# Four graph layers: edge attributes turned in the GCN stages, reciprocals turned instead of sums, query scores as rows, another order of steps

## The chip, the cores and the metric

The kernel runs on one core of a Trainium2 chip. The metric is device time in microseconds, lower is better. The kernel before takes 4228.95 us (median of 3 runs, 4228.57 to 4229.52). A profiled execution has every instruction of the five engines: PE (TensorE), DVE (VectorE), ACT (ScalarE), POOL (GpSimd) and SP (SyncE, which here only issues DMAs).

## The reference

50,000 nodes of 128 features and 25,000 edges, sorted by destination, pass through four layers, each followed by a residual and a layer norm. Only the last two are touched in their arithmetic:

```
# layer 2 (8 heads)
q, k, v = x @ Wq + bq, x @ Wk + bk, x @ Wv + bv
score = einsum('ehd,ehd->eh', q[dst], k[src]) / sqrt(HD) + edge_attr_32 @ We + be
exp_s = exp(score - segment_max(score)[dst])
out = segment_sum(exp_s / (segment_sum(exp_s)[dst] + 1e-8) * v[src]) @ Wo + bo
x = layernorm(x + layernorm(out + x) * gamma + beta)
# layer 3 (4 heads)
alpha = (q_s[dst] + k_s[src] + edge_attr_64 @ We3) / sqrt(C) + gate * edge_weight
ex = exp(leaky_relu(alpha) - segment_max)
x = layernorm(x + segment_sum(ex / (denom[dst] + 1e-16) * v[src]) + bias)
```

Layer 1 is a graph convolution of three rounds (gather, sum by destination, matrix product, relu).

## The kernel before

The program is a row of stages with a barrier of all engines between them. The first two (to about 1800 us) treat all nodes and layer 0. Then come three **graph stages** (`for layer in range(3)`, L1488) and two **attention stages** (`for kind in (2, 3)`, L1713). All five walk over the same 49 chunks of 512 edges (`G_CH`), the tile being 128 partitions x 512 columns of float32.

In a graph stage POOL gathers the source rows of a chunk by four indirect DMAs (L1563), PE turns them (L368, four 128x128 transposes against the identity), DVE runs the segmented scan (L1655) and adds the node's own row, ACT applies the relu, PE multiplies by the next weight. The order there is written out by hand: one iteration `t` issues the work of several chunks, each at its own distance behind `t`.

An attention stage is a software pipeline. `Line` holds five sets of buffers (`RING = 5`). A step such as `maximum` is a function of the chunk L with a **place**, a number in the table `plan`. Every engine sorts its own steps by place + lag x L and issues them in that order, whatever their cost (`Line.run`):

```
order = [(place + self.lag * L, k, L, step) for k, (place, step) in enumerate(self.queue) for L in range(G_CH)]
for when, k, L, step in sorted(order, key=lambda o: o[:3]):
    step(L)
```

So the table alone decides what stands before what on an engine, and it says nothing of when it runs: that is decided by semaphore waits at the head of the instructions. With a lag of 138 (kind 2) or 137 (kind 3), places that differ by one lag are one chunk apart.

The steps of kind 2, in the order of one chunk: `load` (SP), `gather` of source and own rows (POOL, eight indirect DMAs, L886), `residual` (POOL, two additions, L1812 and L1813), `turn_x` (PE: turns source rows, own rows and the edge attributes `ea`), `copy_xT` (ACT, three copies PSUM to SBUF), `products` (PE: keys and queries), `copy_z` (ACT), `qk` (DVE), `scores` (PE: edge term L1895, then sum over heads L1897), `maximum` (DVE: running maximum L919 and what the exponentials need), `exps` (ACT, L929 and L931), `values` (PE, L1887), `sums` (DVE: message, running sum `den` L943, running sum `num` L946), `turn_sums` (PE: turns `num`; four small products with the turned query `xdT` for the scores of the next layer, L1922; four for the rows of `den`, L951), `divide` (DVE), `turn_o` (PE: the quotient turned back), `copy_oT` (ACT), `rows_o` (PE, times Wo, L374), two layer norms on DVE and ACT (`d`, `e`), `store` (SP), `turn_q` and `copy_q` (the result turned for the next chunk's query scores).

Kind 3 has one gather a chunk (four DMAs), no second norm, and at its end `scatter` (POOL, four indirect DMAs to `out`, L1828). Its ACT switches its function table twice a chunk: square root for the norm, exponential for the weights.

PSUM has eight banks of 2 KB a partition, `K[0]` to `K[7]`; a step that writes a bank waits for the reader of its last use.

## Time and profile before

| | us |
|---|---|
| median of 3 runs | 4228.95 |
| profiled execution | 4232.34 |
| its span in the trace | 4230.3 |
| graph stages, from first memset to the start of kind 2 | 1809.7 to 2687.4 |
| kind 2, from its first DMA to the first DMA of kind 3 | 2687.4 to 3578.6 |
| kind 3 | 3578.6 to 4230.3 |
| granted TensorE clock, mean over the span | 0.738 |

A timeline row gives start, duration, engine, line, operation, and in brackets how long the engine sat idle before it and who ended that. Distances from one start to the next are shorter than the durations, since neighbours overlap at their ends.
### The profile page before, as it was taken

How to read it: one execution, taken by the hardware profiler on the slowest of the kernel's cores; microseconds unless marked ns; L12 is line 12 of the kernel's file. 1: busy time of each engine (PE TensorE's matmuls, PEld its weight loads, DVE VectorE, ACT ScalarE, POOL GpSimd, SP SyncE). 2: the span in 40 equal slices, each digit the busy share in tenths (PEclk: the TensorE clock that was granted, in tenths of full speed). 3: DMA queues.
4: the chain of work that ended last, by engine and by line, in shares of the span. 5: the costliest groups of instructions: out<-in, count | busy, mean ns of one | idle time of the engine just before them, and what ended most of it. 6: DMA issues, size and time to landing. Idle time of an engine off the chain costs nothing. (4 is left out here: it accounts for less than half of the span.)

```text
span 4230.3 us, 49000 instructions
## 1 busy us (share of the span) xinstructions
PE 2899.9 (69%) x12128; PEld 1933.6 (46%) x12128; DVE 3478.3 (82%) x8156; ACT 2509.0 (59%) x5535; POOL 2568.4 (61%) x2300
## 2 busy tenths in 40 slices
PE   5877777777742788745465455478888885777775
PEld 3555455554530344444455344345555554444443
DVE  4999999999986888668788699677777785788886
ACT  3777777777751666635545444356666564565555
POOL 6666666666501666167577577587666651666664
PEclk9899999999975777667657655677777785655655
DMA  4887766665534888457667566322222221333331
GB/s 117 182 184 192 188 180 193 183 192 188 174 138 122 253 249 254 150 176 245 220 199 242 196 184 198 94 73 69 64 66 66 69 55 38 102 87 91 91 94 49
DMA packets 390823, 624.83 MB, mean 148 GB/s; under 512 B 125015, under 2 KB 206080, under 8 KB 390542
## 3 DMA queue, kind: packets, MB, share of 16 engines
q1 hardware_dynamic: 320782, 508.68, 40.0%
q0 software_dynamic: 69760, 113.02, 11.4%
q8 instruction: 101, 1.65, 0.2%
q14 instruction: 180, 1.47, 0.1%
HBM read 338.14 MB, written 287.17 MB: 148 GB/s over the span
## 5 line engine op out<-in xcount | busy, mean ns | idle before, releaser
L1563 POOL DMA_INDIRECT gs_g<-table_xw,slot_idx x588 | 616.8, 1049 | 319.5 <-issue 261.9
L886 POOL DMA_INDIRECT gs_t<-table_x,slot_idx x392 | 418.4, 1067 | 302.3 <-issue 198.9
L493 POOL DMA_INDIRECT gs<-x,src_idx x200 | 223.9, 1119 | 292.2 <-DMA xd_rows<-gd 211.0
L368 PE MATMUL ps<-ident,gs_g 128*128 128x128 f32 x588 | 143.4, 391 | 369.1 <-DMA gs_g<-table_xw,slot_idx 369.0
L1258 POOL DMA_INDIRECT slot_idx<-node_map,src_idx x200 | 242.1, 1211 | 196.9 <-DMA slot_idx<-node_map,src_idx 103.6
L481 POOL DMA_INDIRECT node_map<-slot_no,end_idx x200 | 302.6, 1513 | 60.9 <-issue 60.0
L1601 ACT ACTIVATE hT_g<-u_g 128x512 f32<-128x512 f32 x147 | 92.4, 629 | 391.5 <-DVE u_g L1662 391.1
L1828 POOL DMA_INDIRECT out<-x_t,end_idx x196 | 205.5, 1049 | 169.4 <-ACT x_t L339 116.7
L368 PEld LDWEIGHTS ps<-ident,gs_g 128*128 128x128 f32 x588 | 95.9, 200 | 408.0 <-issue 344.6
L1655 DVE TENSOR_TENSOR_SCAN agg_g<-same_seg,agg_g,ps 128x512 f32<-128x512 uint8 x147 | 187.8, 1278 | 93.1 <-PE ps L368 92.5
L493 POOL DMA_INDIRECT gd<-x,dst_idx x200 | 218.7, 1093 | 60.9 <-issue 59.7
L1887 PE MATMUL ps<-xsT_t,Wv 128*128 128x512 f32 x196 | 156.1, 890 | 132.3 <-DVE msg_t L939 132.1
L886 POOL DMA_INDIRECT own_t<-table_x,own_idx x196 | 200.9, 1025 | 59.7 <-issue 59.7
L1650 DVE SCALAR_TENSOR_TENSOR own_g<-bs_row,root,own_g 128x128 f32<-128x128 f32 x588 | 166.7, 345 | 27.6 <-DMA own_g<-table_xw 26.7
L1979 ACT COPY xsT_t<-ps 128x512 f32<-128x512 f32 x49 | 28.7, 585 | 249.3 <-PE ps L368 249.3
L374 PE MATMUL ps<-WS,hT_g 128*128 128x128 f32 x784 | 163.1, 378 | 9.6 <-ACT xw_g L1609 9.3
L594 ACT ACTIVATE x_b<-v_b,nm,rs 128x128 f32<-128x128 f32 x392 | 156.6, 495 | 17.1 <-DVE nm L769 17.1
L368 PE MATMUL ps<-ident,own_g 128*128 128x128 f32 x588 | 146.5, 398 | 29.0 <-DVE own_g L1650 28.0
L594 ACT ACTIVATE x_b<-s_b,nm,rs 128x128 f32<-128x128 f32 x392 | 156.7, 496 | 14.1 <-DVE nm L769 14.1
L374 PEld LDWEIGHTS ps<-WS,hT_g 128*128 128x128 f32 x784 | 154.9, 293 | 11.8 <-issue 11.2
L1952 ACT COPY xsT_t<-ps 128x512 f32<-128x512 f32 x98 | 56.4, 576 | 172.8 <-PE ps L368 172.8
L594 ACT ACTIVATE x_b<-t_b,nm,rs 128x128 f32<-128x128 f32 x392 | 157.4, 510 | 0.0
(365 smaller groups left out, 9936.3 us busy)
## 6 DMA issues: line engine op xcount, KB each, us to landing
table_xw<-xw_b SPq DMA_DIRECT2D x147, 512.0 KB, 4.6
table_x<-x_b SPq DMA_DIRECT2D x98, 512.0 KB, 2.8
own_g<-table_xw SPq DMA_DIRECT2D x147, 256.0 KB, 4.2
x_in<-x SPq DMA_DIRECT2D x49, 512.0 KB
y_g<-table_x SPq DMA_DIRECT2D x49, 512.0 KB, 4.8
table_xw<-xw_g SPq DMA_DIRECT2D x98, 256.0 KB, 2.8
out<-y_g SPq DMA_DIRECT2D x49, 512.0 KB, 4.2
pen_t<-pen_row SPq DMA_DIRECT2D x98, 256.0 KB, 4.1
```

The lines of the kernel that those rows point to most:

```text
L368: last = nc.tensor.transpose(to[0:width, j * P:(j + 1) * P], t[:, j * width:(j + 1) * width], ident[:])
L374: last = nc.tensor.matmul(to[:, j * D:(j + 1) * D], tT[:, j * P:(j + 1) * P], W[:], start=True, stop=bias_row is None)
L481: pool.indirect_dma_start(out=node_map, out_offset=bass.IndirectOffsetOnAxis(ap=end_idx[:, t:t + 1], axis=0), in_=slot_no[:, t:t + 1], in_ ...
L493: pool.indirect_dma_start(out=to[k % 3][:, j * D:(j + 1) * D], out_offset=None, in_=x, in_offset=bass.IndirectOffsetOnAxis(ap=of[:, n:n + ...
L594: last = nc.scalar.activation(to[:, k * D:(k + 1) * D], of(k), ACT.Identity, scale=r[:, n, k:k + 1], bias=b[:, n, k:k + 1])
L886: pool.indirect_dma_start(out=self.B[L % RING][g][:, t * D:(t + 1) * D], out_offset=None, in_=table, in_offset=bass.IndirectOffsetOnAxis(a ...
L1258: pool.indirect_dma_start(out=slot_idx[:, t:t + 1], out_offset=None, in_=node_map, in_offset=bass.IndirectOffsetOnAxis(ap=src_idx[:, t:t + ...
L1563: pool.indirect_dma_start(out=gs[c % 6][:, j * D:(j + 1) * D], out_offset=None, in_=tables[layer], in_offset=bass.IndirectOffsetOnAxis(ap= ...
L1650: V.scalar_tensor_tensor(out=blk, in0=bs_row[layer][:], scalar=root4[:, k:k + 1], in1=blk, op0=ALU.mult, op1=ALU.add).then_inc(S("own_bias ...
L1655: V.tensor_tensor_scan(agg[t % 3][:], same_seg[:, t * CH:(t + 1) * CH], T_X[t % 2], agg[(t - 1) % 3][:, CH - 1:CH], ALU.mult, ALU.add).the ...
L1828: pool.indirect_dma_start(out=out, out_offset=bass.IndirectOffsetOnAxis(ap=end_idx[:, k:k + 1], axis=0), in_=B[L % RING]["x4"][:, t * D:(t ...
L1887: nc.tensor.matmul(K[3], (Wv if kind == 2 else Wv3)[:], B[L % RING]["xsT"][:], start=True, stop=True).then_inc(S("v_ps"), 1)
```

## The change

1. **Edge attributes.** In the three graph stages every third iteration also takes one chunk of the edge attributes: SP loads both kinds (32 and 64 wide) side by side, PE turns them in four transposes (banks 6 and 7, unused there), ACT copies them out with a stride, SP stores the turned chunk to `eaT_d`. The attention stages load `eaT` straight from it; their turn on PE, copy on ACT and the buffers `ea` are gone.
2. **Reciprocals turned (kind 2).** `turn_sums` makes only the rows of `den`. DVE forms the reciprocal (`divisor`), ACT widens it from 32 to 512 columns (`widen_rd`), PE turns it (`turn_rd`), and DVE multiplies it with `num` where that lies, straight into `xsT` (`divide`). The turn of `num`, `turn_o` and `copy_oT` are gone.
3. **Query scores as rows.** Eight instructions (L1922) in `turn_sums` and a copy on DVE (L2062) become `query` (one product of 4x512), `keep_q` (ACT) and `store_q` (SP). The turning of all scores at the start of kind 3 is gone.
4. **Residual.** In kind 2 the two additions go from POOL to DVE.
5. **Banks.** In kind 3 the edge scores and the values have two banks each.
6. **Both plans** get other places; the lags stay.

```diff
+            ea_in = [... f"ea_in_g{layer}_{k}", [P, SUB, 96] ... for k in range(3)]
+            ea_t = [... f"ea_t_g{layer}_{k}", [96, CH] ... for k in range(2)]
+            def ea_chunk(t):
+                return t // 3 if t % 3 == 1 and 0 <= t // 3 < N_E else None
...
+                        k = ea_chunk(t)                      # SP
+                            if k >= 3:
+                                sp.wait_ge(S("ea_ps"), k - 2)
+                            sp.dma_start(ea_in[k % 3][:, :, 0:32], ea_rows(ea32, k))...
+                            sp.dma_start(ea_in[k % 3][:, :, 32:96], ea_rows(ea64, k))...
...
+                        k = ea_chunk(t - 2)                  # PE, ahead of the layer's product
+                            pe.wait_ge(S(f"ea_in{k % 3}"), 32 * (k // 3 + 1))
+                            for j in range(SUB):
+                                last = nc.tensor.transpose(T_E[k % 2][0:96, j * P:(j + 1) * P], ea_in[k % 3][:, j, :], ident[:])
...
+                            nc.scalar.copy(ea_t[k % 2].rearrange("f (p j) -> f j p", j=SUB), ...)
...
-                "turn_x": (38, "xsT_ps xdT_ps eaT_ps"), "copy_xT": (66, "xsT xdT eaT"), "products": (84, "k_ps q_ps"),
+                "turn_x": (-37, "xsT_ps xdT_ps"), "copy_xT": (62, "xsT xdT"), "products": (78, "k_ps q_ps"),
...
-                **ln_plan("f", 474, 490, 516, 522), "scatter": (540, "")}
+                **ln_plan("f", 429, 473, 479, 602), "scatter": (612, "")}
...
-                        sp.dma_start(b["ea"].rearrange("p (j f) -> p j f", j=SUB), hop.rows(ea, L, 0))...
+                        sp.dma_start(b["eaT"][0:width, :], turned[:, L * CH:(L + 1) * CH])...
...
-                        turn(pe, K[2], b["ea"], width).then_inc(S("eaT_ps"), 1)
...
+                        @step("scores_e")
+                            step.due_dma(pe, "ea_in", L)
+                            step.due(pe, "M", L, 1)
+                            step.due(pe, "dz", L, 1)
+                            nc.tensor.matmul(K[2], we2_rep[:], b["eaT"][:], start=True, stop=False)
...
+                        @step("turn_rd")
+                            step.due(pe, "rd_wide", L)
+                            turn(pe, K[4], B[L % RING]["rd_wide"]).then_inc(S("rdT_ps"), 1)
...
+                            nc.tensor.matmul(K[6][0:4, :], q3_cols[:], B[L % RING]["xdT"][:], start=True, stop=True).then_inc(S("q3_ps"), 1)
...
                     @step("turn_sums")
-                        step.due(pe, "num", L)
...
+                            step.due(pe, "rd", L, 1)
+                            step.due(pe, "den", L)
...
+                        @step("widen_rd")
+                            step.due(act, "rd", L)
+                            nc.scalar.copy(b["rd_wide"]..., by_row(b["rd"][:], D // heads)).then_inc(S("rd_wide"), 1)
...
+                        @step("keep_q")
+                            step.due(act, "q3_ps", L)
+                            nc.scalar.copy(B[L % RING]["q"][:], K[6][0:4, :]).then_inc(S("q_kept"), 1)
...
+                            V.tensor_tensor(b["xsT"][:], K[4], b["num"][:], ALU.mult).then_inc(S("oT"), 1)
...
+                        @step("residual")
+                            V.tensor_tensor(rows4(b["xo"][:]), rows4(b["own"][:]), each_row(bo), ALU.add).then_inc(S("xo"), 1)
+                            V.tensor_tensor(rows4(b["w"][:]), rows4(b["own"][:]), each_row(beta2), ALU.add).then_inc(S("x2b"), 1)
```

**PE in kind 2**, one chunk in the middle of the stage (the last digit is the buffer set; `kb_t` holds the quotient before and the widened reciprocal now). Before:

```order
L368 MATMUL ps<-ident,num_t_2 128x128 x4
L1922 MATMUL ps<-q_cols,xdT_t_4 128x4 x4
L951 MATMUL ps<-sel,den_t_2 128x8 x4
L1895 MATMUL ps<-eaT_3,we_rep 128x512
L1897 MATMUL ps<-qk_t_3,head_sum 128x512
L368 MATMUL ps<-ident,kb_t_2 128x128 x4
L368 MATMUL ps<-ident,msg_t_0 128x128 x4
L374 MATMUL ps<-Wo,xsT_t_2 128x128 x4
L368 MATMUL ps<-ident,gs_t_4 128x128 x4
L368 MATMUL ps<-ident,own_t_4 128x128 x4
L368 MATMUL ps<-ident,ea_4 32x128 x4
```

And with the change:

```order
L1932 MATMUL ps<-eaT_3,we_rep 128x512
L375 MATMUL ps<-Wo,xsT_t_1 128x128 x4
L1909 MATMUL ps<-xsT_t_3,Wk 128x512
L1910 MATMUL ps<-xdT_t_3,Wq 128x512
L952 MATMUL ps<-sel,den_t_2 128x8 x4
L1939 MATMUL ps<-qk_t_3,head_sum 128x512
L1963 MATMUL ps<-xdT_t_4,q_cols 4x512
L369 MATMUL ps<-ident,gs_t_4 128x128 x4
L369 MATMUL ps<-ident,own_t_4 128x128 x4
L369 MATMUL ps<-ident,kb_t_2 128x128 x4
L369 MATMUL ps<-ident,msg_t_0 128x128 x4
```

Between `den` and the sum over heads nothing stands any more; the edge term has moved ahead of them, and the query product behind.

**DVE in kind 2**, from `qk` of a chunk to the running maximum of that chunk. Before:

```order
L2045 SCALAR_TENSOR_TENSOR qk_t_2<-ps,bq,kb_t_2 128x512
L2062 COPY q_all<-ps 128x4x4
L959 TENSOR_SCALAR dn_t_1<-ps 128x32
L961 RECIPROCAL rd_t_1<-dn_t_1 128x32
L964 TENSOR_TENSOR kb_t_1<-ps,rd_t_1 128x512
L329 RECIPROCAL rs_t_0<-sd_t_0 128x4
L332 SCALAR_TENSOR_TENSOR nm_t_0<-st_t_0,rs_t_0 128x4
L917 COPY M_t_2<-M_t_1 128x1
```

And with the change:

```order
L2082 SCALAR_TENSOR_TENSOR qk_t_2<-ps,bq,kb_t_2 128x512
L320 BN_STATS st_t_0<-F_t_0 128x6 x2
L2122 TENSOR_TENSOR xo_t_2<-own_t_2,bo 128x512
L2123 TENSOR_TENSOR w_t_2<-own_t_2,beta 128x512
L960 TENSOR_SCALAR dn_t_1<-ps 128x32
L962 RECIPROCAL rd_t_1<-dn_t_1 128x32
L330 RECIPROCAL rs_t_0<-sd_t_0 128x4
L333 SCALAR_TENSOR_TENSOR nm_t_0<-st_t_0,rs_t_0 128x4
L918 COPY M_t_2<-M_t_1 128x1
```

Three 512-wide instructions now stand between `qk` and the maximum that waits for PE's answer to it, where one stood.

**ACT in kind 3**, one chunk. Before:

```order
L1969 ACTIVATE kb_t_3<-ps 128x512
L324 ACT_TABLE_LOAD
L324 ACTIVATE sd_t_1<-st_t_1,eps 128x4
L1952 COPY xsT_t_4<-ps 128x512
L1959 COPY eaT_4<-ps 64x512
L339 ACTIVATE x_t_1<-u_t_1,nm_t_1,rs_t_1 128x128 x4
L929 ACT_TABLE_LOAD
L929 ACTIVATE p_t_3<-p_t_3 128x512
L931 ACTIVATE F_t_3<-F_t_3 128x512
```

And with the change:

```order
L2002 ACTIVATE kb_t_3<-ps 128x512
L1987 COPY xsT_t_4<-ps 128x512
L340 ACTIVATE x_t_0<-u_t_0,nm_t_0,rs_t_0 128x128 x4
L325 ACT_TABLE_LOAD
L325 ACTIVATE sd_t_1<-st_t_1,eps 128x4
L930 ACT_TABLE_LOAD
L930 ACTIVATE p_t_3<-p_t_3 128x512
L932 ACTIVATE F_t_3<-F_t_3 128x512
```

The norm is applied (`x_t`) one chunk later, so its scale is the one made in the cycle before, and the square root and both table loads stand directly ahead of the exponentials.

## Rows read from the trace of the kernel before

**Rows 1.** Graph 1, kinds 2, 3: busy us (count) of PE, PEld, DVE, ACT, POOL; PEclk.
```profile
2110.00:2400.00 290.00, 159.99 (x784) 143.34 (x784) 230.15 (x462) 157.13 (x461) 207.47 (x195) 0.67 0.67 219
2800.00:3500.00 700.00, 580.32 (x2367) 374.38 (x2366) 540.44 (x981) 427.67 (x817) 448.34 (x405) 0.75 0.25 65
3700.00:4150.00 450.00, 339.64 (x943) 194.86 (x942) 371.92 (x650) 263.23 (x433) 299.82 (x287) 0.60 0.34 91
```
**Rows 2.** By source line: first and last start of `qk`, kinds 2 and 3.
```profile
L2045 DVE SCALAR_TENSOR_TENSOR qk_t<-ps,bq,kb_t x49: 724/750/752, 2705.0 to 3530.2; 128x512 f32<-128x512 f32 x49
L2049 DVE SCALAR_TENSOR_TENSOR qk_t<-kb_t x49: 662/674/693, 3605.2 to 4196.5; 128x512 f32<-128x512 f32 x49
```
**Rows 3.** Who waited for whom, 2740 to 3520 (total us, times, longest).
```profile
DVE q_all L2062 <- PE ps L951: 86.1, 44, 3.5
DVE M_t L917 <- PE ps L1897: 70.9, 43, 2.4
```
**Rows 4.** Timeline of DVE in kind 2, one chunk.
```profile
3105.39 0.17 DVE L2062 COPY q_all<-ps 128x16 f32<-128x16 f32 x1 [1.50 <-PE ps L951]
...
3109.03 0.15 DVE L917 COPY M_t<-M_t 128x1 f32<-128x1 f32 x1 [1.97 <-PE ps L1897]
...
3122.58 0.17 DVE L2062 COPY q_all<-ps 128x16 f32<-128x16 f32 x1 [1.50 <-PE ps L951]
```
**Rows 5.** Timeline of PE in kind 2, the same chunk and the next.
```profile
3111.44 1.91 PE L374 MATMUL ps<-Wo,xsT_t 128*128 128x128 f32 x8
3113.15 1.06 PE L368 MATMUL ps<-ident,gs_t 128*128 128x128 f32 x4
3114.00 1.06 PE L368 MATMUL ps<-ident,own_t 128*128 128x128 f32 x4
...
3116.97 1.02 PE L1875 MATMUL ps<-xdT_t,Wq 128*128 128x512 f32 x2
3117.83 1.13 PE L1887 MATMUL ps<-xsT_t,Wv 128*128 128x512 f32 x2
3120.20 0.65 PE L368 MATMUL ps<-ident,num_t 128*128 128x128 f32 x4 [1.24 <-DVE num_t L946]
3120.69 0.95 PE L1922 MATMUL ps<-q_cols,xdT_t 128*128 128x4 f32 x8
3121.50 1.04 PE L951 MATMUL ps<-sel,den_t 128*128 128x8 f32 x8
...
3124.22 2.08 PE L1897 MATMUL ps<-qk_t,head_sum 128*128 128x512 f32 x2
3126.09 1.06 PE L368 MATMUL ps<-ident,kb_t 128*128 128x128 f32 x4
```
**Rows 6.** Groups by form, 2720 to 3500: count, busy us, mean ns, idle before.
```profile
L922 DVE TENSOR_TENSOR F_t<-pen_t,M_t 128x512 f32<-128x512 f32 x45 | 50.2, 1115 | 0.0
...
L1979 ACT COPY xsT_t<-ps 128x512 f32<-128x512 f32 x45 | 26.3, 585 | 228.7 <-PE ps L368 228.7
```
**Rows 7.** Groups by form, 3620 to 4150.
```profile
L2098 DVE TENSOR_TENSOR xo_t<-own_t,bias 128x512 f32<-128x512 f32 x42 | 28.7, 684 | 0.0
```
**Rows 8.** Timeline of DVE in kind 3: the wait of each chunk.
```profile
3868.70 0.69 DVE L939 SCALAR_TENSOR_TENSOR msg_t<-ps,p_t 128x512 f32<-128x512 f32 x1 [1.89 <-ACT p_t L929]
```
**Rows 9.** Timeline of ACT in kind 3, ahead of that.
```profile
3865.07 1.65 ACT L339 ACTIVATE x_t<-u_t,nm_t,rs_t 128x128 f32<-128x128 f32 x4 [0.69 <-DVE nm_t L332]
3866.74 1.28 ACT L929 ACT_TABLE_LOAD   x1
```
**Rows 10.** Timeline of POOL in kind 3.
```profile
3817.67 1.02 POOL L1828 DMA_INDIRECT out<-x_t,end_idx  x1 [1.98 <-ACT x_t L339]
...
3830.14 1.02 POOL L1828 DMA_INDIRECT out<-x_t,end_idx  x1 [1.98 <-ACT x_t L339]
```
**Rows 11.** Timeline of DVE at the start of kind 3.
```profile
3589.04 0.99 DVE L2024 TENSOR_TENSOR qe<-qe,q_sum 128x800 f32<-128x800 f32 x1 [4.15 <-DMA qe<-q_slots]
```
**Rows 12.** Waits in graph stage 1, 2130 to 2390: total, times, longest.
```profile
PE ps L368 <- DMA gs_g<-table_xw,slot_idx: 100.5, 42, 6.1
```

More of the change, by code:

```diff
@@ L1527, in _ @@
                 def _(sp):
-                    for t in range(G_CH + 8):
+                    for t in range(G_CH + 9):
                         if live(t):
@@ L1554, in _ @@
                         landed(sp, "y_out", 5, k)
+                    for k in range(N_E - 2, N_E):
+                        landed(sp, "ea_out", 2, k)
                 @block.gpsimd
@@ L1727, in build @@
         else:
             lag, plan = HOP5_LAG, {
-                "load": (1, "ea_in pen_in ew_in q_in own_in"),
-                "turn_x": (72, "xsT_ps eaT_ps"), "copy_xT": (100, "xsT eaT"), "residual": (105, "xo"), "products": (136, "z_ps"),
-                "gather": (-420, ""), "values": (163, "v_ps"), "copy_z": (174, "kb"), "qk": (218, "zl"),
-                "maximum": (227, "M_first M dz Dm0 Dm"), "exps": (261, "p F"), "sums": (286, "msg den num"),
-                "turn_sums": (342, "num_rows"), "divide": (403, "dn rd divided"), "x4_pre": (416, "x4_pre"),
@@ L1734, in build @@
-                **ln_plan("f", 474, 490, 516, 522), "scatter": (540, "")}
+                "load": (-20, "ea_in pen_in ew_in q_in own_in"),
+                "turn_x": (20, "xsT_ps"), "copy_xT": (28, "xsT"), "residual": (254, "xo"), "products": (80, "z_ps"),
+                "gather": (-420, ""), "values": (142, "v_ps"), "copy_z": (147, "kb"), "qk": (152, "zl"),
+                "maximum": (204, "M_first M dz Dm0 Dm"), "exps": (228, "p F"), "sums": (272, "msg den num"),
+                "turn_sums": (326, "den_rows"), "divide": (361, "dn rd divided"), "x4_pre": (406, "x4_pre"),
@@ L1855, in _ @@
                         b = B[L % RING]
-                        step.due_dma(pe, "ea_in", L)
                         step.due(pe, "kb" if kind == 2 else "xsT", L, 1)
@@ L1914, in _ @@
                             step.due(pe, "e_out", L)
-                            pe.wait_ge(S("oT"), min(L + 3, G_CH))
-                            step.due(pe, "x3T", L, 1)
+                            step.due(pe, "q_kept", L, 1)
                             turn(pe, K[6], B[L % RING]["xn"]).then_inc(S("x3T_ps"), 1)
-                        def query_cols(L):
+                        @step("query")
+                        def _(L):
                             step.due(pe, "x3T", L)
-                            for j in range(SUB):
-                                last = nc.tensor.matmul(K[5][:, 32 + 4 * j:36 + 4 * j], B[L % RING]["xdT"][:, j * P:(j + 1) * P], q3_cols[:], start=True, stop=True)
-                            return last
+                            nc.tensor.matmul(K[6][0:4, :], q3_cols[:], B[L % RING]["xdT"][:], start=True, stop=True).then_inc(S("q3_ps"), 1)
                     @step("turn_sums")
@@ L1927, in _ @@
                         b = B[L % RING]
-                        step.due(pe, "num", L)
-                        step.due(pe, "divided", L, 1)
                         if kind == 2:
-                            step.due(pe, "q_kept", L, 4)
-                        turn(pe, K[4], b["num"])
-                        if kind == 2 and L >= 3:
-                            query_cols(L - 3)
-                        den_rows(pe, K[5], b["den"], sel8 if kind == 2 else sel4, heads).then_inc(S("num_rows"), 1)
-                    step.run()
-                    if kind == 2:
-                        pe.wait_ge(S("divided"), G_CH)
-                        for L in range(G_CH - 3, G_CH):
-                            step.due(pe, "q_kept", L, 1)
-                            query_cols(L).then_inc(S("last_cols"), 1)
+                            step.due(pe, "rd", L, 1)
+                            step.due(pe, "den", L)
+                        else:
+                            step.due(pe, "num", L)
+                            step.due(pe, "divided", L, 1)
+                            turn(pe, K[4], b["num"])
+                        den_rows(pe, K[5], b["den"], sel8 if kind == 2 else sel4, heads).then_inc(S("den_rows"), 1)
+                    step.run()
                 @block.scalar
@@ L1975, in _ @@
                     if kind == 2:
-                        @step("copy_oT")
+                        @step("widen_rd")
                         def _(L):
-                            step.due(act, "oT_ps", L)
-                            nc.scalar.copy(B[L % RING]["xsT"][:], K[6]).then_inc(S("oT"), 1)
+                            b = B[L % RING]
+                            step.due(act, "rd", L)
+                            step.due(act, "qk", L)
+                            nc.scalar.copy(b["rd_wide"].rearrange("p (n c) -> p n c", c=D // heads), by_row(b["rd"][:], D // heads)).then_inc(S("rd_wide"), 1)
                         @step("copy_q")
@@ L2109, in _ @@
                     step.run()
-                    if kind == 2:
-                        for L in range(G_CH - 3, G_CH):
-                            v.wait_ge(S("last_cols"), L - G_CH + 4)
-                            keep_query(L)
             all_meet()
```

153 lines of the change are left out of this document (88 added, 65 removed).

## The prediction

> **What bounds the kernel now.** I read the busy shares by stretch first, then who waited for whom, then one chunk of each attention stage on the timeline.
>
> No engine is full in any stage. In kind 2 PE is busy 580 of 700 us at a mean clock of 0.75, DVE 540; in kind 3 DVE is busy 372 of 450 [rows 1]. So the pace comes from waits. It is (3530.2 - 2705.0) / 48 = 17.19 us a chunk in kind 2 and (4196.5 - 3605.2) / 48 = 12.32 in kind 3 [rows 2].
>
> In kind 2 DVE stands still twice a chunk, 1.50 us for the rows of `den` and 1.97 for the scores [rows 4]; over the stage that is 86.1 and 70.9 us [rows 3]. Both waits are one path. PE has waited 1.24 us for `num`, then does its turn, the query columns, the rows of `den`, the edge term and the sum over heads, 5.9 us from 3120.20 to the last start's successor at 3126.09 [rows 5], and only then can DVE take the next maximum. `num` is the last thing DVE makes from that maximum, so DVE and PE take turns: a ring of maximum, sums, PE, maximum.
>
> In kind 3 DVE waits 1.89 us a chunk for the exponential `p` [rows 8]. ACT is late because the norm's four pieces (1.65) and a table load (1.28) stand directly ahead of it, and that norm waits for DVE [rows 9]. POOL waits 1.98 for the same norm [rows 10].
>
> The graph stages are paced by POOL: 195 gathers take 207.47 us in 290 [rows 1] and PE waits 100.5 us for them [rows 12].
>
> **Kind 2.** The ring opens: the rows of `den` no longer wait for `num`, and the edge term and the query product leave the stretch between them and the scores. What is left as a bound is each engine's own work and PE's clock.
>
> DVE: its busy time is 540.44 / 700 x 17.19 = 13.27 us a chunk [rows 1]. It gains two additions of 0.684 [rows 7], so 1.37, and loses the query copy, 0.17 [rows 4]. It also loses a stretch: the subtraction at L922 takes 1115 ns on average here [rows 6] and an addition of the same size takes 684 in kind 3 [rows 7], 0.43 of difference, and the stage's only POOL arithmetic goes. Sum: 13.27 + 1.37 - 0.17 - 0.43 = 14.0 us. The multiplication by the reciprocal stays at one instruction.
>
> The Trainium skill says in "SBUF — State Buffer", section "SBUF: two separate sides", that a VectorE instruction with two SBUF inputs and a GpSimd instruction that reads SBUF lock each other out for a whole instruction. The row agrees in kind, but its mean price is 0.43 us, less than a whole instruction; by the rule at its fullest the floor would fall by some 0.8 us a chunk more, 40 us in all. I keep to the row.
>
> PE: between the start of a product of 512 columns and the next the rows show 1.87 us at 1.2 GHz (L1897) and 0.86 at 2.4 (L1875), for four turns 0.85 (L368 own rows to their predecessor) and 0.49 (`num`), for the product with Wo 1.71 at 1.2 [rows 5]; halved that is 0.9. The `den` rows take 1.0 at 2.4 [rows 5], so at most 2.0 at 1.2; I take 1.6. A chunk now has four turns, six products of 512 columns with their two halves, one Wo and one `den`: 4 x 0.86 + 6 x 1.87 + 1.7 + 1.6 = 17.9 us at 1.2 and 4 x 0.45 + 6 x 0.87 + 0.9 + 1.0 = 8.9 at 2.4. Before it has two turns more and the query columns for the query product: 19.3 and 9.8. At a clock that is high half of the time (0.75, rows 1) the second gives 1 / (0.5/9.8 + 0.5/19.3) = 13.0, and 14.25 is measured as busy (580.32 / 700 x 17.19); with the same proportion the first gives 11.9 x 14.25 / 13.0 = 13.0 busy. PE then waits about 1.5 us a chunk, for `den` and for `qk`, where it now waits 2.9.
>
> ACT: `copy_oT` and the edge copy go, the widening and the 4-row copy come, two of about 0.585 [rows 6] for two. The widening reads SBUF with a repeated column, which no row shows; between 0.585 and twice that, I take 0.6. ACT has 270 us idle in 700 [rows 1], yet it is on a path: query product, 4-row copy, widening, norm, exponentials, x copies, then PE's products. At 1.2 GHz that path with PE's three products behind it comes to 15 to 16 us a chunk, at 2.4 to 12.
>
> So the floor is 14.0 (DVE), the paths through PE lie at 12 to 16 by the clock. I take **14.5** us a chunk: 48 x (14.5 - 17.19) = **-129 us**. A chunk passes more of the order: the last step lies 537 places behind `qk` where it lay 454, 0.6 of a chunk, so the drain grows by 0 to 9 us; I take **+5**.
>
> **Kind 3.** ACT has the norm of one chunk earlier ready and does both table loads while DVE makes the maximum: `p` needs no more than its own 0.6 after DVE's subtraction, and 3 us of DVE work stand between. The wait of 1.89 goes, and DVE needs 12.47 - 1.89 = 10.6 us, 12.47 being the distance of POOL's two scatters [rows 10]. Next is POOL, with eight indirect DMAs a chunk: 12.47 - 1.98 + 0.30 (the gap it always leaves between two) = 10.8. So POOL ends last, I take 10.85: 48 x (10.85 - 12.32) = **-71 us**. The dropped turn and copy of the attributes, and the second banks, are covered by that. SP's load now waits for a norm issued nearer to it; PE has most of a chunk until it needs the data, so I cost it at nothing; if that cover went, a landing of 2 to 4 us would show in each chunk.
>
> The start of kind 3 loses the turning and storing of scores: DVE's wait for them is 4.15 us [rows 11], and the first attribute turn goes too. **-6**, between 0 and -10.
>
> **Graph stages.** 49 times come four turns on PE (at most 1.06, rows 5), one ACT copy (0.585, or twice that for its stride) and three DMAs. PE and ACT are idle for 130 us in 290 [rows 1] and wait for gathers; POOL paces with (207.47 / 195 + 0.30) x 4 = 5.5 us a chunk. Below nothing it can't be. From above: 49 x 1.06 = 52 us if every turn showed. The DMA engines are 0.67 busy there, and the last digit of POOL's price may grow with them. I take **+6**.
>
> **Sum**, against the profiled execution: 4232.34 - 129 + 5 - 71 - 6 + 6 = 4037. The runs' median lies 3.4 below the profiled one: **4034**.
>
> **The rivals.**
>
> *The clock falls.* With less work PE waits oftener in proportion, and kind 3 shows what that does: busy 340 of 450 at a clock of 0.60 [rows 1]. At 0.60 (high a fifth of the time) PE's work is 1 / (0.2/8.9 + 0.8/17.9) = 14.9 us, 16.3 with the proportion above, and as PE would then hardly wait, the pace 16.4: kind 2 gives 38 instead of 129. Time 4034 + 91 = 4125. For it: kind 3. Against it: PE would be busy nearly all the time, more than the 83% at which it has 0.75 now.
> The Trainium skill, "TensorE: Matmul & The Clock Gate", section "HAM oscillation — how this bites in real kernels", says that waits between pieces of work can bring each following piece back to the half clock. By that rule this rival's time would hold; the two stretches of rows 1 agree in direction.
>
> *Everything hidden.* Kind 2 runs at DVE's 14.0, no drain, nothing in the graph stages: 4034 - 24 - 5 - 6 = 3999.
>
> *The new order does not do what it says in kind 3*: SP's load, the norm's wait or PE's new order brings back a wait of the same size, so the pace stays: 4034 + 71 = 4105. For it: five buffer sets must hold a chunk from load to norm. Against it: each wait I followed is met more than a microsecond early.
>
> *Slower: the graph stages stall on the new loads.* PE works in order, and the attribute turn waits for two DMAs of 128 and 256 B pieces; behind it stand the layer's product and the next chunk's turns, and POOL's gathers wait for those. PE's longest wait for a gather is 6.1 us [rows 12]. Were such a wait added to each of the 49, it would be 300 us: 4034 + 300 = 4334. It decides from 195 / 49 = 4.0 us a time. Against it: the loads are issued two chunks (11 us) ahead.
>
> **Chances.** Forecast 0.62, everything hidden 0.14, clock 0.13, kind 3 unchanged 0.08, slower 0.02, nothing moves 0.01. The range 3975 to 4135 takes in the first four; the forecast's own is 4000 to 4075. A change below 0.2% (8 us) couldn't be told from none. Faster 0.97, same 0.01, slower 0.02.
>
> **What would show it.** `qk` to `qk` 14 to 15 us in kind 2, with DVE's waits for L951 and L1897 (now L952, L1939) together under 30 us, and L922's successor near 690 ns; 10.7 to 11 us in kind 3 with POOL leaving 0.30 between all its DMAs and no wait of DVE for `p`; graph stages within 10 us of before. I am wrong on kind 2 if its clock is below 0.65 and the pace over 15.5, and on kind 3 if POOL still waits for the norm.

## The result, and the profile after

The changed kernel takes **4005.1 us** (median of 4 runs, 3999.41 to 4018.42) against 4228.76 of the kernel before, measured beside it (median of 4); the ratio is 0.9478, 95% interval 0.9462 to 0.9493. The forecast was 4034. The profiled execution took 4018.42 us, its span is 4016.7, the mean granted clock 0.771.

| | before | after | difference | forecast |
|---|---|---|---|---|
| up to the graph stages | 1809.7 | 1807.4 | -2.3 | 0 |
| graph stages | 877.7 | 885.8 | +8.1 | +6 |
| kind 2: first DMA to first `qk` | 17.6 | 19.0 | +1.4 | 0 |
| kind 2: 48 distances of `qk` | 825.2 | 647.7 | -177.5 | -129 |
| kind 2: last `qk` to kind 3 | 48.4 | 41.0 | -7.4 | +5 |
| kind 3: start, to first `qk` | 26.6 | 21.3 | -5.3 | -6 |
| kind 3: 48 distances of `qk` | 591.3 | 552.8 | -38.5 | -71 |
| kind 3: last `qk` to the end | 33.8 | 41.7 | +7.9 | 0 |

Two terms were missed by much, with opposite signs: kind 2 gave 48.5 us more than forecast, kind 3 32.5 less; the others together gave 2.6 more. Against the profiled execution the forecast was therefore 19 us too high (4037 to 4018.4), and against the median 29, since this profiled execution lies 13.3 above its median where I had allowed 3.4.

First the two `qk` lines, first and last start (answer to [rows 2]):

```profile
L2082 DVE SCALAR_TENSOR_TENSOR qk_t<-ps,bq,kb_t x49: 744/751/752, 2712.2 to 3359.9; 128x512 f32<-128x512 f32 x49
L2086 DVE SCALAR_TENSOR_TENSOR qk_t<-kb_t x49: 658/665/693, 3422.2 to 3975.0; 128x512 f32<-128x512 f32 x49
```

That is 13.49 us a chunk in kind 2 (17.19 before) and 11.52 in kind 3 (12.32). Next the busy times by stretch, columns as in [rows 1]; kind 3 is shown in two parts, since its 48 distances are of two sorts:

```profile
2110.00:2400.00 290.00, 162.71 (x848) 143.25 (x848) 228.50 (x462) 171.46 (x477) 204.24 (x195) 0.70 0.76 240
2740.00:3340.00 600.00, 495.39 (x1937) 253.35 (x1936) 575.87 (x1105) 464.00 (x881) 384.09 (x356) 0.89 0.30 82
3450.00:3620.00 170.00, 132.78 (x369) 78.45 (x368) 166.47 (x302) 113.35 (x181) 136.30 (x110) 0.66 0.37 97
3640.00:3940.00 300.00, 200.14 (x512) 119.08 (x510) 239.81 (x428) 156.39 (x259) 242.36 (x190) 0.61 0.33 91
```

In kind 2 DVE is busy 576 of 600 us: it bounds the stage. In the first part of kind 3 DVE is busy 166 of 170 us. The first 20 distances are fast: 7.7 and 9.4 us, then 18 of 10.26. From 3620 on most come 11.9 and 13.7 apart in turn, DVE is busy only 240 of 300, and POOL issues without a stop. PE's clock in kind 2 rose from 0.75 to 0.89 at the same busy share, 83% (580 of 700 and 495 of 600).

DVE's two waits of [rows 3] are gone from kind 2; what is left there, 2740 to 3340:

```profile
DVE qk_t L2082 <- PE ps L1910: 7.7, 14, 0.7
DVE p_t L2138 <- ACT p_t L340: 4.8, 13, 0.4
```

Now POOL in the slow part of kind 3, timeline (start, duration, idle before):

```profile
3703.06 0.98 POOL L1870 DMA_INDIRECT out<-x_t,end_idx  x1 [0.31 <-issue]
3704.35 0.98 POOL L1870 DMA_INDIRECT out<-x_t,end_idx  x1 [0.30 <-issue]
3705.63 1.04 POOL L887 DMA_INDIRECT gs_t<-table_x,slot_idx  x1 [0.30 <-issue]
3706.98 1.01 POOL L887 DMA_INDIRECT gs_t<-table_x,slot_idx  x1 [0.31 <-issue]
3708.30 1.21 POOL L887 DMA_INDIRECT gs_t<-table_x,slot_idx  x1 [0.30 <-issue]
3709.81 1.42 POOL L887 DMA_INDIRECT gs_t<-table_x,slot_idx  x1 [0.30 <-issue]
3711.54 1.54 POOL L1870 DMA_INDIRECT out<-x_t,end_idx  x1 [0.30 <-issue]
3713.39 1.65 POOL L1870 DMA_INDIRECT out<-x_t,end_idx  x1 [0.30 <-issue]
3715.34 1.07 POOL L1870 DMA_INDIRECT out<-x_t,end_idx  x1 [0.30 <-issue]
```

and DVE in the same microseconds:

```profile
3701.92 0.69 DVE L925 TENSOR_TENSOR F_t<-F_t,M_t 128x512 f32<-128x512 f32 x1
3705.96 0.18 DVE L330 RECIPROCAL rs_t<-sd_t 128x4 f32<-128x4 f32 x1 [3.35 <-ACT sd_t L325]
...
3707.35 0.68 DVE L2150 TENSOR_TENSOR xo_t<-own_t,bias 128x512 f32<-128x512 f32 x1
...
3709.15 1.27 DVE L944 TENSOR_TENSOR_SCAN den_t<-F_t,den_t,p_t 128x512 f32<-128x512 f32 x1
3710.34 1.26 DVE L947 TENSOR_TENSOR_SCAN num_t<-F_t,num_t,msg_t 128x512 f32<-128x512 f32 x1
3711.52 0.66 DVE L2086 SCALAR_TENSOR_TENSOR qk_t<-kb_t 128x512 f32<-128x512 f32 x1
...
3712.94 1.28 DVE L920 TENSOR_TENSOR_SCAN M_t<-pen_t,M_t,qk_t 128x512 f32<-128x512 f32 x1
...
3715.59 0.69 DVE L925 TENSOR_TENSOR F_t<-F_t,M_t 128x512 f32<-128x512 f32 x1
```

Read the two side by side. While DVE stands still (3702.6 to 3706) an indirect DMA takes POOL 0.98 to 1.04 us. While DVE runs scans and additions whose inputs all lie in SBUF, the same instruction often takes 1.2 to 1.65, elsewhere up to 2.0, but not always: the one at 3715.34 takes 1.07. That looked like the reason why POOL's price had grown (1051 and 1040 ns before, 1235 and 1324 here), and the first experiments asked whether it is.

### The profile page after: what moved, and what is told of

It reads as the page before. It is cut to its first block and busy times, and to the rows that moved or that the text cites. A ratio compares the mean times of both kernels' runs of the same rounds, so it can differ in the third digit from the quotient of the medians.

```text
span 4016.7 us, 47929 instructions
## 1 busy us (share of the span) xinstructions
PE 2714.8 (68%) x11434; PEld 1743.1 (43%) x11434; DVE 3454.9 (86%) x8203; ACT 2524.7 (63%) x5535; POOL 2514.4 (63%) x2202
## 3 DMA queue, kind: packets, MB, share of 16 engines
q0 software_dynamic: 69760, 113.02, 12.1%
## 5 line engine op out<-in xcount | busy, mean ns | idle before, releaser
L887 POOL DMA_INDIRECT gs_t<-table_x,slot_idx x392 | 449.9, 1148 | 314.5 <-POOLq L83 120.2
L369 PE MATMUL ps<-ident,gs_g 128*128 128x128 f32 x588 | 133.7, 371 | 253.4 <-DMA gs_g<-table_xw,slot_idx 253.3
L1870 POOL DMA_INDIRECT out<-x_t,end_idx x196 | 240.1, 1225 | 61.6 <-issue 58.8
L887 POOL DMA_INDIRECT own_t<-table_x,own_idx x196 | 218.1, 1113 | 59.7 <-issue 59.7
L1987 ACT COPY xsT_t<-ps 128x512 f32<-128x512 f32 x98 | 56.5, 576 | 224.4 <-PE ps L369 224.4
L369 PE MATMUL ps<-ident,gs_t 128*128 128x128 f32 x392 | 77.4, 331 | 142.3 <-DMA gs_t<-table_x,slot_idx 114.1
L369 PEld LDWEIGHTS ps<-ident,own_g 128*128 128x128 f32 x588 | 95.7, 194 | 170.8 <-DVE own_g L1696 170.5
L952 PEld LDWEIGHTS ps<-sel,den_t 128*128 128x128 f32 x784 | 146.8, 272 | 36.6 <-issue 36.6
L369 PEld LDWEIGHTS ps<-ident,gs_t 128*128 128x128 f32 x392 | 54.5, 170 | 248.8 <-issue 248.8
```

The costliest lines, as they stand in the source:

```text
L369: last = nc.tensor.transpose(to[0:width, j * P:(j + 1) * P], t[:, j * width:(j + 1) * width], ident[:])
L887: pool.indirect_dma_start(out=self.B[L % RING][g][:, t * D:(t + 1) * D], out_offset=None, in_=table, in_offset=bass.IndirectOffsetOnAxis(a ...
L952: last = nc.tensor.matmul(to[:, j * heads:(j + 1) * heads], den[:, j * P:(j + 1) * P], sel[:], start=True, stop=True)
L1870: pool.indirect_dma_start(out=out, out_offset=bass.IndirectOffsetOnAxis(ap=end_idx[:, k:k + 1], axis=0), in_=B[L % RING]["x4"][:, t * D:(t ...
```

## Experiments on POOL's price in kind 3

Theory A: DVE's instructions with two inputs in SBUF hold up POOL's issue. Theory B: the queue or the other transfers do.

**1. F in PSUM** (L944, L947 and L925 then read one of their two inputs from PSUM), and **2. the leaky maximum too**:

```diff
-                    b["o"] = b["kb"]
+                    b["o"], b["F"] = b["kb"], K[2]
# in 2 also
-  V.scalar_tensor_tensor(out=b["qk"][:], in0=b["kb"][:], scalar=0.2, in1=b["kb"][:],
+  V.scalar_tensor_tensor(out=b["qk"][:], in0=Z[L % 2], scalar=0.2 * 32.0 ** -0.5, in1=b["kb"][:],
```

> The changed kernel, with the factor F of kind 3 kept in a free PSUM bank instead of SBUF. Nothing else moves. In the changed kernel kind 3 runs 20 chunks at 10.27 us each (DVE busy 58.75 of 60 us) and then at about 12.8, where PE waits for gathers and POOL issues one DMA after the other, at 1.54 us each with its gap of 0.30, against 0.99 + 0.30 when DVE stands still. Theory A (DVE's instructions with two inputs in SBUF hold up POOL's issue): of DVE's 7.9 us of such instructions a chunk, 3.2 (L925, L944, L947) lose the second SBUF input, so about 40% of the stretch of 2.0 us a chunk goes; POOL's mean issue falls to about 1.15, the fast part of the stage lasts some 34 chunks, and the whole is about 40 us faster. Theory B (the queue or the transfers are the limit): issue stays at 1.25, no change within 8 us.

> As the kernel with F in PSUM, and the leaky maximum of kind 3 (L2086) reads one input from the PSUM bank Z instead of the same SBUF tile twice: another 0.67 us a chunk of DVE work with two SBUF inputs goes. Theory A: about half of the stretch goes, mean issue near 1.12, some 8 to 10 us faster than with F alone. Theory B: no change within 8 us.

Measured: 3964.13 us for the first (ratio to before 0.9375, 0.9354 to 0.9395; the changed kernel 0.9478), so 41 us faster than the changed kernel, as theory A said; 3968.67 for the second (0.9381, 0.9362 to 0.9399), no further gain. Kind 3 of the first ran 26 chunks fast and then at about 11.3; POOL's groups in its slow part, 3640 to 3860, are the first pair here (count, busy us, mean ns, idle before), and those of the second kernel, same stretch, follow:

```profile
L1870 POOL DMA_INDIRECT out<-x_t,end_idx x79 | 90.9, 1151 | 24.1 <-issue 24.1
L887 POOL DMA_INDIRECT gs_t<-table_x,slot_idx x76 | 81.8, 1076 | 23.2 <-issue 23.2
```
```profile
L1870 POOL DMA_INDIRECT out<-x_t,end_idx x77 | 89.8, 1166 | 23.5 <-issue 23.5
L887 POOL DMA_INDIRECT gs_t<-table_x,slot_idx x78 | 83.9, 1075 | 23.8 <-issue 23.5 <-ACT x_t L340 0.3
```

The misses: I had expected 34 fast chunks, and a gain from L2086, the leaky maximum, which read one SBUF tile twice. The total doesn't move, but the traces show that the second read did hold POOL up. Here is an issue that starts inside L2086 in run 1, then one at the same distance in run 2:

```profile
3708.65 0.66 DVE L2086 SCALAR_TENSOR_TENSOR qk_t<-kb_t 128x512 f32<-128x512 f32 x1
3708.97 1.23 POOL L1870 DMA_INDIRECT out<-x_t,end_idx  x1 [0.30 <-issue]
```
```profile
3712.33 0.66 DVE L2086 SCALAR_TENSOR_TENSOR qk_t<-ps,kb_t 128x512 f32<-128x512 f32 x1
3712.65 1.00 POOL L1870 DMA_INDIRECT out<-x_t,end_idx  x1 [0.30 <-issue]
```

Between 3500 and 3900 the issues that start well inside L2086 are 0.24 us longer than undisturbed ones in run 1 (26 of them) and 0.02 in run 2 (29). What run 2 saves there it pays at the scan L920: POOL's next issue now starts 0.2 us earlier in it and is 0.89 us longer instead of 0.68. So theory A's count of instructions was right and its forecast of the time wrong.

**3. Loads for five chunks only.** The other transfers of the stage are taken away from the sixth chunk on:

```diff
+                        if kind == 3 and L >= RING:
+                            return                      # load(L) issues nothing
```

> The changed kernel with SP's loads of kind 3 (attributes, pen, weights, query scores, own rows) made for the first five chunks only; the later chunks compute with the data of those. Theory A: POOL's mean issue in kind 3 stays at 1.25, time within 8 us of the changed kernel. Theory B (the other transfers of the stage slow the queue of the indirect DMAs): the issue falls back to 1.05, pace 10.8 or less, 35 us faster or more.

Measured: 4007.67 us (0.9479, 0.9458 to 0.9501), the changed kernel's time. The stage keeps its two parts, 20 fast chunks and then a slow pace. In 3640 to 3940 the queues move 40 GB/s instead of 91, and POOL's mean price falls only from 1.28 to 1.19 us, not to 1.05:

```profile
L1875 POOL DMA_INDIRECT out<-x_t,end_idx x101 | 121.1, 1199 | 30.8 <-issue 30.8
L890 POOL DMA_INDIRECT gs_t<-table_x,slot_idx x101 | 119.4, 1182 | 30.8 <-issue 30.8
```

So the transfers are not what raised the price, though the 0.09 may be theirs.

**4. The price by itself**, where POOL also issues without a stop and had a mean of 1.05:

```diff
+  for extra in (pr_o, pr_q):
+      V.tensor_tensor(extra[:], pr_a[:], pr_b[:] if layer == 0 else T_O[c % 2], ALU.add)
```

> The changed kernel with two extra additions of 128x512 on DVE in every chunk of the first two graph stages, into scratch tiles; in the first stage both inputs lie in SBUF, in the second one of them in PSUM. Theory A: POOL's mean issue, 1.055 us in both before, rises in the first stage (by the 0.25 us of stretch per us of such DVE work seen in kind 3: 1.3 us / 4 gathers x 0.25 = 0.08, so 1.14) and stays within 0.02 in the second. Theory B: the same in both. The stages get longer in both, since DVE is 80% busy there and gets 1.3 us more a chunk of 5.5.

POOL's gathers in the first graph stage (two SBUF inputs) and in the second (one in PSUM):

```profile
L1595 POOL DMA_INDIRECT gs_g<-table_xw,slot_idx x193 | 220.7, 1144 | 58.8 <-issue 58.2 <-PE ps L369 0.3 <-DMA gs_g<-table_xw,slot_idx 0.3
```
```profile
L1595 POOL DMA_INDIRECT gs_g<-table_xw,slot_idx x196 | 207.3, 1057 | 102.6 <-issue 57.9 <-POOLq L83 43.1 <-PE ps L369 1.2
```

1144 ns against 1057, with the same number of added instructions of the same size. This shows theory A: it is where the second input lies. The single run took 4055 us, with DVE busy 203 of 210 us in the first of these stages.

Issue by issue the traces are sharper than the mean. An issue that starts inside a DVE instruction with two SBUF inputs is longer by what is left of that instruction, less 0.1 to 0.2 us. In the first stage of run 4 (1850 to 2060) the seven issues that start with 0.41 to 0.43 us of an added addition left take 1.29 or 1.30 us; in the second (2150 to 2380) all 42 that start inside one take 1.00 or 1.01. Five issues of the first stage that start early in the first of the two additions wait for the second one too (1.82 to 2.07 us). In the kind 3 lines above, the issue at 3713.39 has 0.83 us of the scan L920 left and takes 1.65 where an undisturbed one takes 0.98; the gather at 3709.81 has 0.61 of L944 left and takes 1.42 instead of 1.02. Who comes first decides: between 3450 and 3940 the 12 issues that start in the first 0.06 us of L944 are not delayed at all, the 14 that start 0.08 to 0.10 us into it by 0.98 to 1.02. So the 0.25 us of delay for each us of such DVE work, which the expectations use, is an average over issues that wait for the rest of one instruction and issues that don't wait.

The Trainium skill, "SBUF — State Buffer", section "SBUF: two separate sides", says that a DVE instruction with two SBUF inputs and a GpSimd instruction that reads SBUF lock each other out for the whole instruction, whichever starts first. The traces agree: an issue that starts 0.08 us into the scan L944 is prolonged by 0.98 to 1.02 us. For the writing of the descriptors of a DMA issued by GpSimd the same section names only DVE's two-port modes, and reports that a `tensor_tensor` did not hold such a DMA up. Here it does (1144 ns against 1057 in run 4), and the measurement decides.

## Experiments on kind 2

**5. Another order for the kernel before**, scores ahead of the turn of sums:

```diff
-  "turn_sums": (255, "num_rows"), "divide": (270, "dn rd divided"), "turn_o": (285, ...
+  "turn_sums": (268, "num_rows"), "divide": (288, "dn rd divided"), "turn_o": (303, ...
   # all later steps + 18
```

> The kernel before with nothing but another order in kind 2: PE makes the scores of the next chunk ahead of the turn of num, the query columns and the rows of den, DVE divides after the next maximum, and all later steps come 18 places later. Every instruction of the kernel before is still there, residual on POOL included. Theory A (in the kernel before, DVE and PE take turns around maximum, sums, turn of sums, scores, so the order alone opens the ring): DVE's wait of 1.97 us for the scores and 1.50 for the rows of den shrink, the pace falls from 17.19 to about 15.5 us, 60 to 100 us faster; the rest of the gain is work that left PE and DVE. Theory B (the pace was PE's amount of work at its clock): within 20 us of before.

Measured: 4331.36 us (1.0251, 1.023 to 1.0273), 100 us slower, which neither theory forecast. **9. The same, done with more care:**

```diff
+  "turn_o": (318, ...), "copy_oT": (325, ...), "rows_o": (333, ...), "h_res": (366, ...),
+  **ln_plan("d", 400, 416, 448, 482), "x3_pre": (507, ...), **ln_plan("e", 525, 555, 571, 621),
```

> The kernel before with another order of kind 2 again, every instruction kept. The first such order put PE's turn of o ahead of the turns of the next chunk's rows, and copy_oT ahead of the exponentials, so DVE stood 4.7 us waiting for the product with Wo. Here the turn of o comes behind the next chunk's turns, copy_oT behind the exponentials, the statistics of the first norm between qk and the maximum, and the roots next to each other. Theory A (order alone opens the ring of maximum, sums, PE, maximum): DVE's waits for scores and den rows fall from 3.5 to about 1.3 us a chunk, pace about 15.5, 60 to 90 us faster than before. Theory B (a ring can't be opened without taking PE work away: four turns, the query columns): pace 16.8 or more, within 20 us of before or slower.

Measured: 4223.77 us (0.999, 0.9979 to 1.0), nothing. Theory A's forecast of the time failed in both; in 9 the time is the one that theory B gave. The waits of DVE in 9, 2800 to 3500 (in all, times, longest):

```profile
DVE F_t L2078 <- PE ps L374: 103.3, 41, 4.3
DVE M_t L917 <- PE ps L1897: 41.9, 41, 1.5
DVE p_t L2086 <- ACT p_t L339: 32.9, 31, 1.1
DVE q_all L2062 <- PE ps L951: 4.8, 9, 0.5
```

The waits for scores and `den` rows did fall, to 46.7 us in 41 chunks, 1.1 each. But a wait of 2.5 for the product with Wo took their place: this order left 0.6 us of DVE work (the scale of two norms) between `divide` and `h_res`, while the turn of `o`, its copy and the product with Wo take 0.66 + 0.58 + 1.16 us at the high clock and 1.06 + 0.58 + 2.08 at the low one. In 5 the same wait was 178.9 us in 36 chunks. Run 9 also settles another rival: PE's granted clock was 0.87 in this stretch against 0.75 in the kernel before, and the pace stayed at (3523.3 - 2696.2) / 48 = 17.23 us, so a higher clock alone gives nothing.

**10. The filler taken away in the changed kernel**:

```diff
-                "load": (1, "ea_in pen_in"), "residual": (129, "xo x2b"),
+                "load": (1, "ea_in pen_in"), "residual": (117, "xo x2b"),
-                **ln_plan("d", 400, ...
+                **ln_plan("d", 392, ...
```

> The changed kernel, with the residual and the statistics of the first norm in kind 2 placed ahead of qk instead of behind it. DVE does the same work; of its 3.2 us between qk and the next maximum 1.05 are left (divisor and scale of a norm), while PE makes the scores. Theory A (DVE's own work between qk and maximum is what hides PE's scores): PE's last product takes 1.1 to 2.0 us and its start 0.2, so DVE waits 0.3 to 1.1 us a chunk for the scores, 15 to 50 us slower than the changed kernel. Theory B (DVE has enough elsewhere): within 8 us.

Measured: 4074.72 us (0.9639, 0.9621 to 0.9657), 70 us slower, more than forecast, by moving three DVE instructions across one. The pace is (3426.2 - 2707.6) / 48 = 14.97 us, and in 2740 to 3340 the old wait is back, with one for ACT behind it:

```profile
DVE M_t L918 <- PE ps L1939: 40.2, 40, 1.5
DVE p_t L2138 <- ACT p_t L340: 28.1, 33, 1.0
```

**6. The wait for `num` put back** in the changed kernel:

```diff
                             step.due(pe, "den", L)
+                            step.due(pe, "num", L)
```

> The changed kernel, with PE's rows of den in kind 2 waiting for num again, as in the kernel before. Theory A' (it is the order that opened the ring, with DVE now full, busy 576 of 600 us): these rows come a stretch of DVE work ahead of where they are needed, the wait is short; within 8 us of the changed kernel. Theory B' (leaving out the wait for num is what opened it): up to 1.3 us a chunk, the length of the scan of num, comes back, 60 us slower.

Measured: 3998.71 us (0.9452, 0.9432 to 0.9473): no cost. In the new order the wait that the change leaves out is worth nothing.

**12. The old way of dividing in the new order** (PE's turn of `num` and of the quotient, the copy on ACT):

```diff
-  "widen_rd": (264, "rd_wide"), "turn_rd": (260, "rdT_ps"), "divide": (303, "oT")
+  "copy_oT": (264, "oT"), "turn_o": (260, "oT_ps"), "divide": (277, "divided")
```

> The changed kernel with the kernel before's way of dividing in kind 2: num turned to rows on PE (four turns more, behind num), DVE divides the rows right behind the divisor, PE turns the result, ACT copies it to xsT where it widened the reciprocals. All else, the places of the order too, is the changed kernel's. The two orders tried on the kernel before gained nothing: the second cut DVE's waits for scores and den rows from 3.5 to 1.1 us a chunk, but 2.5 us came back in DVE's wait for the product with Wo, behind divide, turn, copy. Theory A (it is the order as a whole, with the divided rows wanted only 60 places later, that opens the path, whatever is turned): DVE stays nearly full, PE's four turns (0.45 to 1.06 us a chunk) go into its idle time; 0 to 30 us slower than the changed kernel. Theory B (turning the reciprocals takes the divide off the path from num to the next maximum, and without it the wait comes back): pace 15.5 or more, 80 us slower or more.

This run came to a slower chip: the kernel before took 4489.6 us there, so the ratio, 0.9611 (0.954 to 0.9682), can't be set against the others. The trace can:

```profile
L2082 DVE SCALAR_TENSOR_TENSOR qk_t<-ps,bq,kb_t x49: 749/751/752, 2982.2 to 3674.9; 128x512 f32<-128x512 f32 x49
```

The first two distances are 18.9 and 45.7 us, with waits in them that the profile puts down to no engine of this core; the other 46 make (692.7 - 64.6) / 46 = 13.65 us. The changed kernel's last 46 make 13.58. The granted clock is 0.94 here and 0.89 there; the fastest chunks take 13.5 us here and 13.2 there. So in the new order the old division costs 0.07 to 0.3 us a chunk, 3 to 14 us in all, and theory A holds for the pace. What the start of the stage would cost on the usual chip is open.

**7. The residual back on POOL:**

```diff
+  nc.gpsimd.tensor_tensor(rows4(b["xo"][:]), rows4(b["own"][:]), each_row(bo), ALU.add)...
-  V.tensor_tensor(rows4(b["xo"][:]), rows4(b["own"][:]), each_row(bo), ALU.add)...
```

> The changed kernel with the two additions of kind 2's residual back on POOL, at the same place of the order. Theory A: DVE is what bounds kind 2 now (96% busy, PE's clock 0.89); 1.37 us a chunk leave it, and if nothing else came the pace would fall from 13.49 to 12.2; but POOL needs 8 x 1.38 + 2 x about 1 us = 13.1 a chunk and its arithmetic and DVE's hold each other up (DVE's L922 1115 ns before against 690 now), so the pace stays within 0.4 us of 13.5 and the time within 20 us of the changed kernel. Theory B (no price for the meeting of POOL and DVE): pace 13.0, 25 us faster. Theory C (the move to DVE was essential): slower by more than 20 us.

Measured: 4024.98 us (0.9525, 0.9506 to 0.9544), 20 us slower; pace (3380.1 - 2710.5) / 48 = 13.95, 0.46 more than the changed kernel's. That is on the border between theories A and C. DVE lost two additions a chunk and is as busy as before: a four-column instruction now stands waiting. Its group in 2760 to 3340, then the same in the changed kernel:

```profile
L333 DVE SCALAR_TENSOR_TENSOR nm_t<-st_t,rs_t 128x4 f32<-128x4 f32 x84 | 71.8, 854 | 2.9
```
```profile
L333 DVE SCALAR_TENSOR_TENSOR nm_t<-st_t,rs_t 128x4 f32<-128x4 f32 x86 | 14.4, 167 | 2.9
```

Two times (854 - 167) is 1.37 us a chunk, just what the two additions cost DVE. The hold-up works in both directions.

## Experiments on the graph stages, and a faster version

**8. No edge turning:**

```diff
-                return t // 3 if t % 3 == 1 and 0 <= t // 3 < N_E else None
+                return None
```

> The changed kernel without the loads, turns, copies and stores of the edge attributes in the graph stages; kinds 2 and 3 load rows of another table of the same shape in their place, so their numbers are not those of the edges. What it takes back is the price of the added work in the graph stages: forecast 6 us, and 8.3 by the comparison of the stages, so 5 to 10 us faster than the changed kernel, all of it in the graph stages. If instead the 8.3 was chance from run to run, no change.

Measured: 3992.28 us (0.9452, 0.943 to 0.9474), 13 us faster than the changed kernel by the medians; the intervals overlap. From the first gather of the graph stages to the first of kind 2 the traces show 871.7 us without and 882.5 with: 11 us. So there is a price; it is a little more than the +8.1 of the table (8.3 in the expectation) and than the 5 to 10 forecast.

**11. A faster version**: F in PSUM, the leaky maximum written back to bank Z (so L920 and L922 read one input from PSUM), the bias of the residual in a free corner of a bank:

```diff
+                    b["o"], b["F"] = b["kb"], K[2]
+  V.scalar_tensor_tensor(out=Z[L % 2], in0=Z[L % 2], scalar=0.2 * 32.0 ** -0.5, in1=b["kb"][:],
+  V.tensor_copy(K[5][:, 256:384], bias3[:])     # once; L2150 reads it
```

> A version meant to be faster: the changed kernel with F of kind 3 in PSUM, the leaky maximum read from and written to the PSUM bank Z (so the scan of the maximum at L920 and the subtraction at L922 have one input there), and the bias of the residual in a free part of a PSUM bank. Of DVE's two-input SBUF work of 7.9 us a chunk 1.4 is left. Theory A: POOL needs 8 x 1.29 + 1.4 x 0.25 = 10.7 us a chunk, its stock of gathered chunks then lasts to the end of the stage, all 48 chunks run at DVE's 10.25; 20 us faster than with F alone, about 3944. Theory B (the leaky maximum's failure to gain shows that the rest is something else): issue stays at 1.12 and the time within 8 us of 3964.

Measured: **3940.65 us** (0.9318, 0.9302 to 0.9334). Its `qk` line, its stretch 3450 to 3860, and POOL there:

```profile
L2090 DVE SCALAR_TENSOR_TENSOR ps<-ps,kb_t x49: 670/671/699, 3419.2 to 3906.9; 128x512 f32<-128x512 f32 x49
```
```profile
3450.00:3860.00 410.00, 300.07 (x884) 167.47 (x883) 401.69 (x724) 270.64 (x441) 318.54 (x301) 0.68 0.39 105
```
```profile
L887 POOL DMA_INDIRECT gs_t<-table_x,slot_idx x151 | 160.5, 1063 | 46.1 <-issue 44.2 <-ACT x_t L340 1.8
L1870 POOL DMA_INDIRECT out<-x_t,end_idx x150 | 158.3, 1055 | 45.7 <-issue 45.1 <-ACT x_t L340 0.3 <-PE ps L369 0.3
```

The mean issue is back at 1.06 us and all chunks come at DVE's own pace, 10.2, as theory A said. This beats the changed kernel by 64 us, with one small copy more at the start and otherwise the same instructions.

## Why the prediction was right, and where it was not

DVE as the bound of kind 2 was right, and POOL as that of kind 3 for its second part. That the sum lies so near is in part luck: kind 2 gave 48.5 us more than forecast and kind 3 32.5 less. The 4005 lies nearer to the rival "everything hidden" (3999) than to 4034, and that is chance too: that rival had kind 2 at 14.0 us a chunk and the graph stages free, and neither came.

**Kind 2, right in place, mis-sized by 48 us.** I said that a ring of maximum, sums, PE, maximum opens and DVE's own work bounds next. Both hold. I put that work at 14.0 us and the pace half a microsecond above; chunks with PE at the high clock run at 13.2, and twelve with PE at a mean clock of 0.76 at 14.35. The largest part of the miss is the stretch that leaves with POOL's additions. I took 0.43 us from L922 alone, but the rows of before show it in three more places, 2720 to 3500:

```profile
L943 DVE TENSOR_TENSOR_SCAN den_t<-F_t,den_t,p_t 128x512 f32<-128x512 f32 x45 | 63.5, 1410 | 0.0
...
L924 DVE TENSOR_TENSOR F_t<-F_t,M_t 128x512 f32<-128x512 f32 x45 | 41.9, 931 | 1.6
L332 DVE SCALAR_TENSOR_TENSOR nm_t<-st_t,rs_t 128x4 f32<-128x4 f32 x89 | 21.0, 236 | 3.0
```

After the change these take 1274, 695 and 168 ns: 0.14 + 0.24 + 2 x 0.07 = 0.5 us a chunk more, 24 us in all. Another 0.2 is that I counted each added addition with its full 0.684 us, while the next instruction starts 0.6 us behind it (L2122, L2123 and L960 at 3062.42, 3063.01 and 3063.61). Another 0.2 is the allowance above the floor, of which 0.3 of 0.5 was needed: I counted on a clock of 0.75 and it rose to 0.89. What is left, 0.1 us, is open. The rival of a falling clock was wrong in sign.

**Why the ring opened.** I named the wait for `num` and the edge term first. Runs 6 and 12 say that in the new order neither the wait nor the form of the division matters, run 10 that three DVE instructions between `qk` and the maximum are worth 70 us, run 7 that the residual on DVE is worth 20, runs 5 and 9 that opening one such place is worth nothing if another closes. So part 6 of the change, the places, is needed for the gain. That it is enough isn't shown: every run with the new order also has the turn of the edge attributes and the query columns off PE, and no run has both back on it.

**Kind 3, half wrong.** "No wait of DVE for `p`" and "POOL leaving 0.30 between all its DMAs" came true. Which part of the change took the wait for `p` away, the order on ACT, the second banks or the edge turn and copy, was not tried apart. The step that failed is the sum 12.47 - 1.98 + 0.30 = 10.8 for POOL: it took POOL's price per DMA as fixed at 1.05 [rows 1, 10]. With DVE busy 98% of the time POOL needs 12.4. It isn't DVE's busy share as such: from 3640 on DVE is busy 80% of the time, less than the 83% before, and POOL pays 1.28 an issue. It is where the issues fall. Before, the same pattern came back every 12.47 us, and POOL's issues mostly started outside DVE's two-input instructions or near their end: the 287 in 3700 to 4150 are on average 0.05 us longer than undisturbed ones, the 190 in 3640 to 3940 after the change 0.28.

And I took the slower engine's pace for all 48 chunks. In fact the gathers made ahead (their place is -420, three lags before the chunk) carried the stage for 20 chunks at DVE's 10.26 (I had DVE at 10.6). The last gather of chunk 9 (counted from 0) ended 36.1 us ahead of that chunk's `qk`, that of chunk 18 only 17.0: 2.1 us less with each chunk, which is 12.4 - 10.26. From chunk 21 on the lead stands at 12.1 us and POOL sets the pace. The two errors partly cancel: 11.52 on average.

**Small terms.** The drain of kind 2 fell by 7.4 us where I had +5. It is a stretch of the same pipeline, so I take it that it shrank with the pace, where I had only counted places; and these I misread: the last step before, `copy_q`, lies 472 places behind `qk`, not 454. The drain of kind 3 grew by 7.9: the norm and the scatter stand 602 and 612 places behind where they stood 522 and 540, about half a chunk, and in run 11, where POOL has no backlog, 37.9 of the 41.7 us remain. The graph stages cost 8 to 11 us, the start of kind 3 gave 5.3, as forecast.

## What to carry to other kernels

An engine's price per instruction holds only as long as its instructions meet the neighbour's in the same way: before using it in a floor, look at the single durations and at what the neighbour was doing when each instruction started. If POOL and DVE share work on SBUF, a new order on DVE can change POOL's price. Where DVE sends something to PE and needs the answer, count the DVE work that the order puts between the two, for every such pair; opening one and closing another gains nothing. If POOL issues DMAs next to a full DVE, try to move one of DVE's two inputs to PSUM: the scan L944 takes 1.27 us with `F` in PSUM and with `F` in SBUF, and issues that start inside it are delayed only in the second case.
